# Storing the query and key parts of the first attention by dimension, batch, head and token

## The chip, the cores and the metric

The kernel runs on one NeuronCore of a Trainium2 chip. The metric is the time of one execution on the device, in microseconds (us). The program is one launch with eight layers behind each other (four attentions and four feed-forward layers); the change touches the first of them only.

## The reference, cut to what matters

Eight batches of 512 tokens with 256 features pass through eight layers. The first layer is a causal attention of 16 heads with 16 dimensions each, with scores that also have a term for the relative position:

```
q = (einsum('bsd,ed->bse', layernorm(x), Wq) + bq)  -> [b, head 16, token 512, dim 16]
k, v likewise from the context
QEr  = einsum('bhsd,ld->bhsl', q, Er)
Srel = _skew(QEr)                       # row s is shifted by s
attn = (einsum('bhsd,bhtd->bhst', q, k) + Srel) / sqrt(16)
attn = softmax(where(causal, attn, -inf))
x = x + tanh(gate) * einsum('bhst,bhtd->bhsd', attn, v)
```

Scores are wanted in float32. The kernel gets this from bfloat16 matmuls: each of q and k is split into three bfloat16 parts whose sum is the float32 number, and six products of parts (the list TERMS: 1·1, 1·2, 2·1, 1·3, 3·1, 2·2) are summed in one matmul with a contraction of 6 × 16 = 96 rows.

## The kernel before

The first layer runs as four phases with a barrier of all engines between two of them.

**qkv, "a0" (lines 133 to 373).** Per batch VectorE normalises the tokens, TensorE turns them and multiplies with the weights, and this gives four tiles of 128 features × 512 tokens (two of k, two of q, the list `jobs`). ScalarE copies each with its bias to `q32`. VectorE (`split`, lines 247 to 261) makes three bfloat16 parts of it in five instructions, in one of two buffers `parts[:, j % 2]`. SyncE (`save`, lines 185 to 194) waits for the parts, stores them to device memory with one DMA, 128 partitions × 3 parts × 512 tokens (384 KB), and later stores the values and loads the next context, in the same queue. VectorE may write a parts buffer again when the store of two tiles before has landed (line 254). The tensors in device memory are `q_parts` and `k_parts`, [3, 512, 4096] in bfloat16; a row is one feature (head × 16 + dimension), and a batch is 512 of its 4096 tokens, so a contiguous run of one head, dimension and batch is 1 KB.

**rel_scores, "r0" (lines 1243 to 1360).** GpSimd (POOL) loads the query parts: for each of the six terms one DMA, 16 partitions (the dimensions) × 16 heads × 512 tokens = 256 KB, into rows 16·i to 16·i + 15 of `Q` (line 1273). The loads of two batches may be under way at a time (`q_free`). TensorE multiplies each head with the table Er, VectorE and ScalarE copy the results to one of four buffers `out`, and SyncE stores each head's 640 KB to `rel` (line 1286). A buffer is filled again when its store has landed (lines 1330 and 1351).

**causal_attention, "t0" (lines 3625 to 3887).** SyncE loads the relative scores of a head skewed, in four DMAs of 64 to 256 KB (`relsb`, line 3715). GpSimd loads the query and key parts, six terms × (Q, K) × 256 KB, again 16 partitions each, and the values V, 13 DMAs a batch (line 3756 and 3752). For batch 0 all 13 are issued at the start; for the others one pair is issued after every second head of the batch before (lines 3760 to 3768). GpSimd also adds the mask to the loaded scores and waits for them (`rel{j}`). TensorE's first score matmul waits for all 13 loads (`loaded`). VectorE adds scores and finds the maximum, ScalarE takes the exponential, TensorE turns the tiles and multiplies them with V.

**outproj, "o0".** It isn't touched.

GpSimd's DMAs go through the queue q0 (software), SyncE's through q1 (hardware); both are served by the same 16 DMA engines. The function `attention` (line 377) is edited too, but `program` doesn't call it.

Of the kernel before, what the change touches and what calls it, by code (L numbers as in the profile page):

```python
# [9 lines left out]
BF16 = mybir.dt.bfloat16  # L10
# [5 lines left out]
P = 128  # L16
NB = 8
S = 512
# [114 lines left out]
def qkv(nc, G, name, src, jobs, weights, vjob, ctx=None, affine=None, tile_k=None, nlog=0):  # L133
# [13 lines left out]
    with phase(nc, name, "w c0 c1 c_free stats rstd xn xn_free xt_ps xt_ps_free xt xt_free "  # L147
# [21 lines left out]
        with nc.Block() as block:  # L169

            @block.sync
            def _(sp):

                for c in ("parts_st0", "parts_st1", "v_st0", "v_st1"):
                    sp.sem_inc(s[c], 16)
                for k, (view, shape) in weights.items():
                    sp.dma_start(W[k][tuple(slice(None) for _ in shape)], view).then_inc(s["w"], 16)

                def load(b, p):
                    if ctx is not None:  # L180

                        sp.wait_ge(s["c_free"], b + 1)
                        sp.dma_start(cT[:, p], ctx.rearrange("(k p) t -> p k t", p=P)[:, :, ds(b * S, S)]).then_inc(s[f"c{p}"], 16)

                def save(b, p):
                    for j, (wn, blk, sc, bias, scale, dst, row) in enumerate(jobs):

                        sp.wait_ge(s["parts"], b * nj + j + 1)
                        alone(sp)
                        sp.dma_start(dst.rearrange("r f t -> f r t")[row:row + P, :, ds(b * S, S)],  # L190
                                     parts[:, j % 2]).then_inc(s[f"parts_st{j % 2}"], 16)

                    sp.wait_ge(s["v_sb"], (b + 1) * NVB)
                    sp.dma_start(vdst.rearrange("(t p) d -> p t d", p=P)[:, ds(b * NT, NT), :], vsb[:, p]).then_inc(s[f"v_st{p}"], 16)

                load(0, 0)
                load(1, 1)
                with sp.Fori(0, NB // 2 - 1) as it:
                    for p in range(2):
                        b = it * 2 + p  # L200
                        save(b, p)
                        load(b + 2, p)
                for p in range(2):
                    save(NB - 2 + p, p)

                sp.wait_ge(s["parts_st0"], 16 + 16 * NB * ((nj + 1) // 2))
                sp.wait_ge(s["parts_st1"], 16 + 16 * NB * (nj // 2))
                for p in range(2):
                    sp.wait_ge(s[f"v_st{p}"], 16 + 16 * NB // 2)

# [14 lines left out]
            @block.vector  # L225
            def _(dve):
                ch = Chain(dve, s["dvc"])
                dve.sem_inc(s["q32_free"], 2)

                def rows(b, p, before):  # L230
                    ch.at(before)
                    for t in range(NT):
                        last = nc.vector.bn_stats(st[:, t, :], src[:, ds(b * NT + t, 1), :].rearrange("p o d -> p (o d)"))
                    ch.link(last)
                    alone(dve)
                    for t in range(NT):
                        last = nc.vector.bn_aggr(mv[:, p, t, :], st[:, t, :])
                    last.then_inc(s["stats"], 1)
                    dve.wait_ge(s["rstd"], b + 1)

                    dve.wait_ge(s["xn_free"], b + 1)
                    for t in range(NT):
                        last = nc.vector.tensor_scalar(xn[:, p, t, :], src[:, ds(b * NT + t, 1), :].rearrange("p o d -> p (o d)"),
                                                       mv[:, p, t, 0:1], rstd[:, p, t:t + 1], ALU.subtract, ALU.mult)
                    last.then_inc(s["xn"], 1)

                def split(b, before):
                    ch.at(before)
                    for j in range(nj):

                        dve.wait_ge(s["q32"], b * nj + j + 1)
                        q = q32[:, j % 2, :]
                        k = (nj + 1 - j % 2) // 2
                        dve.wait_ge(s[f"parts_st{j % 2}"], b * (16 * k) + 16 * (j // 2) + 16)
                        ch.link(nc.vector.tensor_copy(parts[:, j % 2, 0, :], q))
                        ch.link(nc.vector.tensor_tensor(r1[:, :], q, parts[:, j % 2, 0, :], ALU.subtract))
                        ch.link(nc.vector.tensor_copy(parts[:, j % 2, 1, :], r1[:, :]))
                        ch.link(nc.vector.tensor_tensor(r2[:, :], r1[:, :], parts[:, j % 2, 1, :], ALU.subtract))
                        ch.link(nc.vector.tensor_copy(parts[:, j % 2, 2, :], r2[:, :]))
                        dve.sem_inc(s["parts"], 1)  # L260
                        dve.sem_inc(s["q32_free"], 1)


                rows(0, 0, 0)
                with dve.Fori(0, NB // 2 - 1) as it:
                    for p in range(2):
                        b = it * 2 + p
                        rows(b + 1, 1 - p, b * link_per_batch + 1)
                        split(b, b * link_per_batch + 2)
                rows(NB - 1, 1, (NB - 2) * link_per_batch + 1)  # L270
                split(NB - 2, (NB - 2) * link_per_batch + 2)
                split(NB - 1, (NB - 1) * link_per_batch + 1)

# [103 lines left out]
def attention(nc, G, name, qs, ks, vs, H, DH, blocks, masks, odst, sums, rel=None):  # L377
# [32 lines left out]
    with phase(nc, name, "in0 in1 loaded qk_free vh vones rel0 rel1 score least expo turned cp_dve cp_act pv "  # L410
# [72 lines left out]
        with nc.Block() as block:  # L483

            @block.gpsimd
            def _(pool):
                with pool.Fori(0, NB // 2) as it:
                    for p in range(2):
# [3 lines left out]
                        for i, (qp, kp) in enumerate(TERMS):  # L492
                            c, r = i // TPC, i % TPC
                            for dst, part, src in ((Q, qp, qs), (K, kp, ks)):
                                pool.dma_start(dst[r * DH:(r + 1) * DH, p, c],
                                               src[part - 1].rearrange("(h d) t -> d h t", d=DH)[:, :, ds(b * S, S)]).then_inc(s[f"in{p}"], 16)
                        pool.dma_start(V[:, p], vs.rearrange("(t p) d -> p t d", p=P)[:, ds(b * NT, NT), :]).then_inc(s[f"in{p}"], 16)

                        pool.wait_ge(s[f"in{p}"], it * (16 * nload) + 16 * nload)
# [743 lines left out]
def rel_scores(nc, G, name, qs, er, rel):  # L1243
# [5 lines left out]
    with phase(nc, name, "er cast erp q0 q1 q_free mm mm_free_a mm_free_v cp_a cp_v st0 st1 st2 st3 dvc") as (s, sb, ps):  # L1249
# [9 lines left out]
        with nc.Block() as block:  # L1259

            @block.gpsimd
            def _(pool):
# [5 lines left out]
                with pool.Fori(0, NB // 2) as it:  # L1268
                    for p in range(2):
                        b = it * 2 + p  # L1270
                        pool.wait_ge(s["q_free"], b + 1)
                        for i, (qp, kp) in enumerate(TERMS):
                            pool.dma_start(Q[i * DH:(i + 1) * DH, p],
                                           qs[qp - 1].rearrange("(h d) t -> d h t", d=DH)[:, :, ds(b * S, S)]).then_inc(s[f"q{p}"], 16)

            @block.sync
            def _(sp):
# [2347 lines left out]
def causal_attention(nc, G, name, qs, ks, vs, rel, odst, sums):  # L3625
# [16 lines left out]
    with phase(nc, name, "in0 in1 loaded rel0 rel1 rel2 rel3 mask masked vones vh score least expo turned cp_dve cp_act pv zero o_free o_st0 o_st1") as (s, sb, ps):  # L3642
# [60 lines left out]
        with nc.Block() as block:  # L3703
# [45 lines left out]
            def _(pool):  # L3749
                def load(p, b, r):  # L3750
# [2 lines left out]
                        return  # L3753
                    qp, kp = TERMS[r]
                    for dst, part, src in ((Q, qp, qs), (K, kp, ks)):
                        pool.dma_start(dst[r * DH:(r + 1) * DH, p], src[part - 1].rearrange("(h d) t -> d h t", d=DH)[:, :, ds(b * S, S)]).then_inc(s[f"in{p}"], 16)

                def batch(it, p, more=True):
                    b = it * 2 + p
# [134 lines left out]
def program(nc, a):  # L3894
    G = Globals()
    with ExitStack() as ctx:
# [11 lines left out]
        G.gate = sb("gate", [P, 8])  # L3908
        G.ones = sb("ones", [1, P])
        G.mhalf = sb("mhalf", [P, 32])  # L3910
        G.qs = dram("q_parts", [3, 512, TOK], BF16)
        G.ks = dram("k_parts", [3, 512, TOK], BF16)
        G.vs = dram("values", [TOK, D])
        G.osT = dram("attended", [D, TOK])
        G.sums = dram("sums", [NB, 16, S])
# [2 lines left out]
        G.kh = dram("k_halves", [2, D, TOK])  # L3918
        G.one_row = dram("one_row", [1, S])
        constants(nc, G, a)  # L3920
        qs, ks = G.qs[:, 0:D, :], G.ks[:, 0:D, :]
        if 0 in STAGES:
            rel = dram("rel", [NB * 16, P * 10 * P])
            qkv(nc, G, "a0", G.X,
# [163 lines left out]
```

## Time and profile before

| | |
|---|---|
| median of 3 runs | 6493.87 us (6456.07 to 6500.29) |
| the profiled execution, own time | 6481.38 us |
| its span (first to last instruction) | 6479.7 us |
| granted TensorE clock, mean | 0.839 |
| PE / DVE / ACT / POOL busy over the span | 72% / 61% / 43% / 31% |
| a0 (projections and splitting) | about 30 to 166 us of the span |
| r0 (relative scores) | about 167 to 459 us |
| t0 (causal attention) | about 459 to 1130 us |

A share of busy time is a mean over the whole program. The change lies in its first 1130 us, so the rows that count are those of windows in this stretch. The DMA share is the mean busy share of the 16 DMA engines.

### The profile page before, as it was taken

Reading aid. Unit: us, or ns where it says so; the run is one execution under the profiler, and the core shown is the slowest. Engines: PE = TensorE matmul, PEld = TensorE weight load, DVE = VectorE, ACT = ScalarE, POOL = GpSimd, SP = SyncE. Lnnn points to the kernel's source line nnn. Section 1 sums busy time; section 2 is a strip of 40 time slices with the busy share of each in tenths; the row PEclk is TensorE's granted clock in tenths of the full one; section 3 lists DMA queues with packets and bytes.
Section 4 is the critical chain, followed back from the end, with each engine's and each line's share of the span. In section 5 each row is a group of like instructions: output and inputs, shape, how many; then the busy total and the mean of one; then the engine's idle time right before and its main releaser. Section 6 shows DMA issues by size and latency. Waiting matters only on the chain. (4 is left out here: it accounts for less than half of the span.)

```text
span 6479.7 us, 102180 instructions
## 1 busy us (share of the span) xinstructions
PE 4692.1 (72%) x24710; PEld 2851.4 (44%) x24710; DVE 3959.5 (61%) x8261; ACT 2814.7 (43%) x5978; POOL 2018.5 (31%) x3020
## 2 busy tenths in 40 slices
PE   7446666391787973797675767697677687995897
PEld 4113333240353322687233645486555574333533
DVE  6335555637546876444387966557866455886565
ACT  2235555114314762322453556434556332772353
POOL 0114443000006641222343554124553113552342
PEclk9557889695897987898777989898889898997897
DMA  4999996100034330210452232002321006332543
GB/s 157 301 323 194 184 185 149 50 0 0 0 115 133 90 75 20 70 43 23 128 157 59 109 113 74 29 7 78 133 74 46 26 16 200 91 86 60 181 124 97
DMA packets 372621, 648.43 MB, mean 100 GB/s; under 512 B 78834, under 2 KB 182931, under 8 KB 372200
## 3 DMA queue, kind: packets, MB, share of 16 engines
q1 hardware_dynamic: 300728, 450.70, 22.9%
q0 software_dynamic: 71488, 193.32, 12.4%
q8 instruction: 133, 2.18, 0.1%
q14 instruction: 272, 2.23, 0.1%
HBM read 373.99 MB, written 238.70 MB: 95 GB/s over the span
## 5 line engine op out<-in xcount | busy, mean ns | idle before, releaser
L1115 DVE TENSOR_REDUCE t_nmax<-t_aps 128x2 f32<-128x1024 f32 x700 | 837.6, 1222 | 281.9 <-PE t_aps L1037 276.4
L1222 ACT ACTIVATE t_expT<-t_bps 128x512 f32<-128x512 f32 x1290 | 701.7, 599 | 288.2 <-PE t_bps L1056 237.8
L1056 PE MATMUL t_bps<-t_Q,t_K 51*128 51x512 f32 (+2 forms) x1290 | 528.9, 472 | 59.4 <-ACT t_expT L1222 43.3
L1037 PE MATMUL t_aps<-t_K,t_Q 49*128 49x512 f32 (+2 forms) x1400 | 467.7, 462 | 64.7 <-DMA t_K<-k_halves 29.4
L1056 PEld LDWEIGHTS t_bps<-t_Q,t_K 51*128 51x128 f32 (+2 forms) x1290 | 230.2, 190 | 528.6 <-ACT t_expT L1222 374.2
L2474 DVE TENSOR_TENSOR f_hl<-f_h,f_hh 128x512 fp32r<-128x512 f32 x192 | 203.9, 1062 | 412.4 <-ACT f_hh L2399 412.4
L3882 ACT ACTIVATE t_relsb<-t_relsb,t_nmax 128x128 f32<-128x128 f32 (+3 forms) x515 | 280.3, 561 | 317.4 <-DVE t_nmax L3855 314.1
L1083 PE MATMUL t_ops<-t_expT,t_V 128*17 128x512 f32 (+1 forms) x2560 | 416.6, 618 | 0.4 <-ACT t_expT L1222 0.4
L3816 PE MATMUL t_tps<-ident,t_relsb 128*128 128x128 f32 x1280 | 266.8, 317 | 173.5 <-ACT t_expT L3701 165.2
L2762 POOL TENSOR_TENSOR a_crossed<-a_qsb,a_tab 128x256 f32<-128x256 f32 x272 | 268.0, 1007 | 299.7 <-ACT a_qsb L2709 272.1
L3855 DVE CUSTOM_DVE_ANT_0 t_relsb<-t_sps,t_relsb 128x128 f32<-128x128 f32 (+3 forms) x515 | 235.5, 485 | 138.2 <-POOL t_relsb L3781 86.5
L3781 POOL TENSOR_TENSOR t_relsb<-t_relsb,t_M 128x128 f32<-128x128 f32 (+1 forms) x384 | 198.9, 547 | 384.8 <-DMA t_relsb<-rel 358.2
L1156 POOL DMA_DIRECT2D t_Q<-q_halves x525 | 272.1, 520 | 141.8 <-POOLq L78 73.3
L3816 PEld LDWEIGHTS t_tps<-ident,t_relsb 128*128 128x128 f32 x1280 | 183.8, 163 | 253.0 <-issue 235.9
L3529 ACT ACTIVATE t_prob<-t_summed,t_nmax 128x256 f32<-128x256 f32 (+1 forms) x560 | 266.0, 480 | 35.3 <-DVE t_nmax L3581 23.4
L1156 POOL DMA_DIRECT2D t_K<-k_halves x525 | 268.7, 514 | 16.4 <-issue 8.9
L3471 PE MATMUL t_tps<-ident,t_prob 128*128 128x128 f32 x964 | 153.9, 306 | 154.3 <-DVE t_prob L3596 154.3
L1037 PEld LDWEIGHTS t_aps<-t_K,t_Q 49*128 49x128 f32 (+2 forms) x1400 | 216.0, 200 | 104.4 <-issue 52.3
L1307 PE MATMUL r_o<-r_erk,r_Q 96*128 96x128 bf16 (+3 forms) x512 | 160.8, 460 | 133.6 <-DVEq L1335 92.4
L3539 ACT COPY t_expT<-t_tps 128x512 f32<-128x512 f32 (+1 forms) x276 | 144.6, 524 | 256.3 <-PE t_tps L3471 256.3
L2339 PE MATMUL f_yps<-f_wdh,f_hh 128*128 128x256 f32 x768 | 217.8, 284 | 13.9 <-DVE f_hl L2474 13.9
L1886 PE MATMUL f1c_ups<-gridT,upT 128*128 x192 | 105.0, 713 | 166.4 <-ACTq L1891 141.0
(431 smaller groups left out, 12493.6 us busy)
## 6 DMA issues: line engine op xcount, KB each, us to landing
rel<-r_out SPq DMA_DIRECT2D x128, 640.0 KB, 5.4
t_relsb<-rel SPq DMA_DIRECT2D x128, 256.0 KB, 4.6
t_Q<-q_halves POOLq DMA_DIRECT2D x420, 64.0 KB, 2.5
t_K<-k_halves POOLq DMA_DIRECT2D x420, 64.0 KB, 2.6
t_relsb<-rel SPq DMA_DIRECT2D x128, 192.0 KB, 3.6
k_halves<-a_parts SPq DMA_DIRECT2D x48, 512.0 KB
q_halves<-a_parts SPq DMA_DIRECT2D x48, 512.0 KB, 5.5
t_relsb<-rel SPq DMA_DIRECT2D x128, 128.0 KB, 3.5
```

The source lines that it names most:

```text
L1037: last = nc.tensor.matmul(aps[:, (t * PPG + i) % 2, x, :], operand(Qr, KA, p, h, slice(t * P, (t + 1) * P)), operand(Kr, KA, p, h, slice(0 ...
L1056: nc.tensor.matmul(bps[:, slot_of(kb, j), :], operand(Kr, KB, p, h, slice(kb * P, (kb + 1) * P)), operand(Qr, KB, p, h, slice(0, S)), star ...
L1083: last = nc.tensor.matmul(ops[j * COL:j * COL + VW, :], V[:, p, kb, g * HG + j, :], expT[:, kb % RING, j, :], start=kb == 0, stop=kb == NT ...
L1115: nc.vector.tensor_reduce(nmax[:, g, t, i * HPT:(i + 1) * HPT], aps[:, (t * PPG + i) % 2], AX.X, ALU.max, negate=True).then_inc(s["maxed"], 1)
L1156: pool.dma_start(dst[o + i * DH:o + (i + 1) * DH, p, cols], rows(src, part, r, g, b)).then_inc(sem, 16)
L1222: nc.scalar.activation(expT[:, kb % RING, j, :], bps[:, slot_of(kb, j), :], ACT.Exp).then_inc(s["expo"], 1 + (PAD if end else 0))
L2339: last = nc.tensor.matmul(o, fast(x), fast(w), start=m == 0 and i == 0 and t % 2 == 0, stop=m == NF - 1 and i == 2, skip_group_check=True)
L2762: last = nc.gpsimd.tensor_tensor(y[:, :, k, :], x[:, :, 1 - k, :], tab[:, 2 * i + 1, t, k * HW:(k + 1) * HW].unsqueeze(1).broadcast_to([P, ...
L3529: nc.scalar.activation(prob[:, u.slot, i, x, 0:w], summed[:, u.slot, i, x, 0:w], ACT.Exp, scale=-1.0, bias=nmax[:, u.slot, i, x:x + 1], ac ...
L3816: last = nc.tensor.transpose(tps[:, u.t % 2, kb * P:(kb + 1) * P], u.tile()[:, kb * P:(kb + 1) * P], G.ident[:, :])
L3855: nc.vector.tensor_tensor_reduce(out=u.tile(), in0=sps[:, u.t, 0:u.w], in1=u.tile(), scale=1.0, scalar=3.0e38, op0=ALU.add, op1=ALU.min, a ...
L3882: nc.scalar.activation(u.tile(), u.tile(), ACT.Exp, scale=-1.0, bias=nmax[:, u.j, u.t:u.t + 1]).then_inc(s["expo"], 1)
```

## The change

The two tensors get the shape [3 parts, 16 dimensions, 8 batches, 16 heads, 512 tokens]. All heads of one dimension and batch now stand behind each other, 16 × 512 × 2 bytes = 16 KB in one piece. A load of one term is then 16 partitions × 8192 elements. The store of a tile, which has 8 heads × 16 dimensions on its 128 partitions, can no longer be written with one access pattern for the three parts, and becomes three DMAs of 128 KB; a run in it is still 1 KB. The semaphores of the stores count 48 a tile where they counted 16.

```
 sp.wait_ge(s["parts"], b * nj + j + 1)
 alone(sp)
-sp.dma_start(dst.rearrange("r f t -> f r t")[row:row + P, :, ds(b * S, S)],
-             parts[:, j % 2]).then_inc(s[f"parts_st{j % 2}"], 16)
+for r in range(3):
+    rows = dst[r].rearrange("d b h t -> b h d t")[ds(b, 1), row // 16:row // 16 + P // 16].rearrange("b h d t -> (b h) d t")
+    sp.dma_start(rows, parts[:, j % 2, r]).then_inc(s[f"parts_st{j % 2}"], 16)
...
-dve.wait_ge(s[f"parts_st{j % 2}"], b * (16 * k) + 16 * (j // 2) + 16)
+dve.wait_ge(s[f"parts_st{j % 2}"], b * (48 * k) + 48 * (j // 2) + 48)
...
 # rel_scores, and likewise causal_attention for Q and K
-pool.dma_start(Q[i * DH:(i + 1) * DH, p],
-               qs[qp - 1].rearrange("(h d) t -> d h t", d=DH)[:, :, ds(b * S, S)]).then_inc(s[f"q{p}"], 16)
+pool.dma_start(Q[i * DH:(i + 1) * DH, p], qs[qp - 1, :, ds(b, 1)].rearrange("d b h t -> d (b h) t")).then_inc(s[f"q{p}"], 16)
...
-G.qs = dram("q_parts", [3, 512, TOK], BF16)
-G.ks = dram("k_parts", [3, 512, TOK], BF16)
+G.qs = dram("q_parts", [3, 16, NB, 16, S], BF16)
+G.ks = dram("k_parts", [3, 16, NB, 16, S], BF16)
```

On SyncE, in the steady loop of a0, a batch before: four stores of parts, then the values and the next context.

```order
L190 DMA k_parts<-a_parts 128x3x512
L188 REGISTER_ALU
L190 ISA
L190 DMA k_parts<-a_parts 128x3x512
L188 REGISTER_ALU
L190 DMA q_parts<-a_parts 128x3x512
L188 REGISTER_ALU
L190 DMA q_parts<-a_parts 128x3x512
```

The same place in the changed kernel:

```order
L192 DMA k_parts<-a_parts 8x16x512
L192 ISA
L192 DMA k_parts<-a_parts 8x16x512
L192 ISA
L192 DMA k_parts<-a_parts 8x16x512
L188 REGISTER_ALU
L192 DMA q_parts<-a_parts 8x16x512 x3
L188 REGISTER_ALU
L192 DMA q_parts<-a_parts 8x16x512 x3
```

Three DMAs stand where one stood, with all else in its place (the second piece begins at the second k tile), and the slowest dimension of the target is 8 (heads) in place of 128.

On GpSimd, the start of t0 before (the first of the six pairs of batch 0, then the end of them with the values):

```order
L3756 DMA t_Q<-q_parts 16x16x512
L3756 DMA t_K<-k_parts 16x16x512
L3752 DMA t_V<-values 128x4x256
```

And in the changed kernel:

```order
L3756 DMA t_Q<-q_parts 16x8192
L3756 DMA t_K<-k_parts 16x8192
L3752 DMA t_V<-values 128x4x256
```

No instruction moved; the shape is one piece of 8192 elements for each of 16 partitions in place of 16 pieces of 512. TensorE, VectorE and ScalarE have the same instructions in the same order.

## Rows read from the trace of the kernel before

**Rows 1.** Stretches of 50 us: busy time by engine, PEclk, DMA share, GB/s.

```profile
core 0: us, PE busy (x) PEld busy (x) DVE busy (x) ACT busy (x) POOL busy (x), PEclk, DMA share, GB/s
100.00:150.00 50.00, 46.33 (x142) 24.38 (x141) 40.13 (x90) 14.70 (x24) 2.76 (x5) 0.93 0.43 139
300.00:350.00 50.00, 28.31 (x91) 9.66 (x92) 20.64 (x47) 17.53 (x47) 3.38 (x6) 0.50 1.02 366
650.00:700.00 50.00, 35.61 (x227) 18.92 (x225) 25.95 (x101) 26.74 (x58) 20.29 (x40) 0.83 0.98 172
```

**Rows 2.** Waits in r0 and, last, in t0: us in total, times, longest.

```profile
ACT r_out L1354 <- DMA rel<-r_out: 157.2, 121, 8.0
PE r_o L1307 <- DMA r_Q<-q_parts: 36.0, 1, 36.0
POOL t_relsb L3781 <- DMA t_relsb<-rel: 287.8, 77, 9.9
```

**Rows 3.** DMA view, 196 to 203 us: only loads of r_Q move.

```profile
DMA packets 249, 0.82 MB, mean 117 GB/s; under 512 B 50, under 2 KB 50, under 8 KB 249
...
q0 software_dynamic: 247, 0.81, 102.2%
q1 hardware_dynamic: 2, 0.01, 1.4%
```

**Rows 4.** DMA view, 205 to 222 us: only stores of rel, from 128 partitions.

```profile
DMA packets 1576, 7.17 MB, mean 422 GB/s; under 512 B 176, under 2 KB 176, under 8 KB 1576
```

**Rows 5.** DMA view, 495 to 500 us in 40 slices: from 497.5 on V and rel.

```profile
DMA  9499829999996979798999799989999999999999
GB/s 213 45 205 139 111 21 152 213 193 188 213 274 188 434 258 451 270 434 299 361 336 369 250 389 332 410 320 357 361 373 332 332 389 336 365 389 373 328 356 426
...
q1 hardware_dynamic: 783, 0.95, 63.3%
q0 software_dynamic: 152, 0.52, 41.0%
```

**Rows 6.** Timeline: start us, us, engine, instruction, idle before it.

```profile
175.72 4.11 POOL L1273 DMA_DIRECT2D r_Q<-q_parts  x7
...
192.93 2.33 PE L1307 MATMUL r_o<-r_erk,r_Q 96*128 96x128 bf16 x8 [36.02 <-DMA r_Q<-q_parts]
...
195.35 42.40 SPq L1286 DMA_DIRECT2D rel<-r_out  x20
...
459.77 0.57 POOL L3756 DMA_DIRECT2D t_Q<-q_parts  x1 [63.94 <-POOLq L78]
...
498.93 1.33 PE L3809 MATMUL t_sps<-t_K,t_Q 96*128 96x128 bf16 x5 [47.69 <-POOLq L3771]
```

**Rows 7.** Exponentials of t0 (L3882) by stretch: ACT busy (x), PEclk, DMA share, GB/s.

```profile
600.00:650.00 50.00, 24.41 (x45) 0.82 0.95 203
650.00:700.00 50.00, 21.31 (x39) 0.83 0.98 172
700.00:750.00 50.00, 22.66 (x43) 0.86 0.89 186
750.00:800.00 50.00, 19.49 (x36) 0.73 0.91 196
800.00:850.00 50.00, 22.00 (x41) 0.86 0.77 170
850.00:900.00 50.00, 21.69 (x40) 0.86 0.95 180
900.00:950.00 50.00, 21.76 (x40) 0.80 0.94 188
1050.00:1100.00 50.00, 24.70 (x46) 0.93 0.55 155
```

**Rows 8.** Groups by line, GpSimd's DMA issues: busy us, mean ns, idle before.

```profile
L1273 POOL DMA_DIRECT2D r_Q<-q_parts x48 | 27.0, 567 | 193.2 <-PEq L1311 192.0 <-issue 0.4
L1267 POOL DMA_DIRECT2D r_erk<-r_pbf x6 | 2.9, 490 | 4.5 <-DVE r_pbf L1321 4.5
```

**Rows 9.** Lines L255 and L190 alone: what VectorE's first cast waits for; the stores.

```profile
  DMA k_parts<-a_parts: 6.0, 15
  DVE a_parts L259: 3.5, 8
...
  DMA q_parts<-a_parts: 0.7, 2
...
L190 SPq DMA_DIRECT2D k_parts<-a_parts x16: 372/372/401, 33.1 to 155.3; - x16
...
DMA to landing us min/median/max: 3.2/3.2/3.9
```

**Rows 10.** DMA view, 117 to 134 us in 40 slices: stores of parts in bursts.

```profile
GB/s 361 267 195 251 328 357 256 15 0 0 0 0 0 0 169 349 349 58 0 0 0 39 342 347 198 0 0 0 0 190 347 347 41 0 0 0 17 332 323 323
```

**Rows 11.** Timeline of a0: VectorE's split beside TensorE, and ScalarE's copy.

```profile
108.09 0.43 DVE L255 CAST a_parts<-a_q 128x512 bf16<-128x512 f32 x1 [0.42 <-DMA k_parts<-a_parts]
...
110.45 1.07 ACT L295 COPY a_xT<-a_xps 128x512 f32<-128x512 f32 x2 [0.23 <-ACT a_vsb L313]
...
111.28 0.43 DVE L255 CAST a_parts<-a_q 128x512 bf16<-128x512 f32 x1 [0.39 <-DMA k_parts<-a_parts]
...
112.80 3.60 PE L356 MATMUL a_jps<-a_xT,a_wq 128*128 128x512 f32 x8
```

More of the change, by code:

```diff
@@ L174, in _ @@
                 for c in ("parts_st0", "parts_st1", "v_st0", "v_st1"):
-                    sp.sem_inc(s[c], 16)
+                    sp.sem_inc(s[c], 48 if c.startswith("parts") else 16)
                 for k, (view, shape) in weights.items():
@@ L204, in _ @@
                     save(NB - 2 + p, p)
-                sp.wait_ge(s["parts_st0"], 16 + 16 * NB * ((nj + 1) // 2))
-                sp.wait_ge(s["parts_st1"], 16 + 16 * NB * (nj // 2))
+                sp.wait_ge(s["parts_st0"], 48 + 48 * NB * ((nj + 1) // 2))
+                sp.wait_ge(s["parts_st1"], 48 + 48 * NB * (nj // 2))
                 for p in range(2):
@@ L495, in _ @@
                                 pool.dma_start(dst[r * DH:(r + 1) * DH, p, c],
-                                               src[part - 1].rearrange("(h d) t -> d h t", d=DH)[:, :, ds(b * S, S)]).then_inc(s[f"in{p}"], 16)
+                                               src[part - 1, :, ds(b, 1)].rearrange("d b h t -> d (b h) t")).then_inc(s[f"in{p}"], 16)
                         pool.dma_start(V[:, p], vs.rearrange("(t p) d -> p t d", p=P)[:, ds(b * NT, NT), :]).then_inc(s[f"in{p}"], 16)
@@ L3755, in load @@
                     for dst, part, src in ((Q, qp, qs), (K, kp, ks)):
-                        pool.dma_start(dst[r * DH:(r + 1) * DH, p], src[part - 1].rearrange("(h d) t -> d h t", d=DH)[:, :, ds(b * S, S)]).then_inc(s[f"in{p}"], 16)
+                        pool.dma_start(dst[r * DH:(r + 1) * DH, p], src[part - 1, :, ds(b, 1)].rearrange("d b h t -> d (b h) t")).then_inc(s[f"in{p}"], 16)
                 def batch(it, p, more=True):
@@ L3920, in program @@
         constants(nc, G, a)
-        qs, ks = G.qs[:, 0:D, :], G.ks[:, 0:D, :]
+        qs, ks = G.qs, G.ks
         if 0 in STAGES:
```

## The prediction, made before the changed kernel ran

> **What bounds the kernel now.** I read the stretches of 50 us first, since the change lies in the first 1130 us only, then the waits in them, then the DMA view of short windows, and the timeline where phases begin. In a0 the DMA engines have room (share 0.43), and TensorE and VectorE are busy for 46 and 40 of 50 us; in r0 the DMA share is 1.02 with TensorE at 28 us; in t0 it is 0.98 in the stretch shown, with no compute engine over 36 us [rows 1]. The waits say the same: in r0 ScalarE waits 157 us for the stores of rel, and TensorE 36 us once for its first query parts; in t0 GpSimd waits 288 of 500 us for the loads of rel [rows 2]. So r0 and t0 are bound by the DMA engines, and the loads that the change reshapes, 48 in r0 and 96 in t0 of 256 KB each, use these engines. The reader is to ask one question: how long does a load hold them, and why?
>
> Alone, the loads move 117 GB/s with the engines' time full (102%), and in the 7 us of that window SyncE's queue moves 2 packets, although its stores are issued from 195.35 us on [rows 3, 6]. Stores of rel alone move 422 GB/s [rows 4]. A load of 262,144 bytes at 117 GB/s holds all 16 engines for 2.24 us. This is the size that the change wants to cut.
>
> **Is it the length of a run?** The change makes runs of 1 KB into runs of 16 KB. If the short run set the 117 GB/s, other transfers with short runs would be slow too. They are not: V goes through the same queue q0, its runs are 256 float32 numbers, also 1 KB, and it lands 128 partitions wide. In the window where it moves (q0's 0.52 MB there are V) beside loads of rel with runs of 512 bytes to 2 KB, the engines reach 332 to 389 GB/s in the steady part [rows 5]. The packets of a query load are also not 1 KB: 0.82 MB in 197 packets of 2 KB or more (249 less 50) is 4.2 KB each, so the trace shows four runs in a packet already [rows 3]. What sets these loads apart is that each writes only 16 partitions, and that their runs in device memory lie 8 KB and 128 KB apart. The first stays in the changed kernel, the second goes. I hold the width for the cause, since it is the only one of the two that a transfer cannot spread over, but the rows don't exclude the other. The Trainium skill, page "SBUF — State Buffer", section "Door 1: The DMA port swizzle", says that the DMA rate depends on how many of 16 ports a transfer's partitions reach, and gives about 109 GB/s as the limit for 16 partitions; by that rule the load stays at 2.4 us whatever its runs are. The trace's 117 GB/s lies close to it, a little above. That page alone can't settle it, since no row here has 16 partitions with long runs.
>
> **The loads, step by step.** The issue on GpSimd: 144 instructions of 567 ns become ones like r_erk's, which have 16 runs and take 490 ns: 144 x 77 ns = 11 us of GpSimd [rows 8]. It counts for nothing, since GpSimd waits 192 us in front of these very issues in r0 [rows 8] and for rel in t0 [rows 2]; without this cover it would be 11 us. The transfers: I take the same 2.24 us, so 0. The bounds are the two rivals below.
>
> **The stores.** One DMA of a tile becomes three. A SyncE issue takes 372 ns, so the last third is issued 0.74 us later; the store lands 3.2 us after its issue now [rows 9]. Its data moves at some 347 GB/s [rows 10], 393,216 bytes in 1.13 us. The trace has no store whose target's slowest dimension is 8. The bounds: if each issue hides under the data of the one before and VectorE's delay under TensorE's slack (below), it costs 0; at the slowest rate of any row, 117 GB/s, the data takes 3.36 us, 2.2 us more, and with the issues the landing is 2.9 us later. I take 1.3 us, near the lower end, because the source stays 128 partitions wide as in the 347 GB/s row. The Trainium skill, page "DMA: Bandwidth & Descriptors", section "Why a DMA increments its semaphore by 16 and not by 1", says that a DMA is spread over the largest number of engines up to 16 that divides the slowest dimension of both sides; that would be 8 here, 1.13 us more per store, and with it 8 x 1.9 = 15 us in place of the 10 below.
>
> Who waits: VectorE's first cast of a tile waits for the store of two tiles before, 17 times in 32, for 6.7 us in all, and when it isn't a store it waits as long for its own chain (3.5 us over 8) [rows 9]. So stores land just in time, in two of four tiles a batch (108.09 and 111.28) [rows 11], and any delay reaches VectorE. A delay of the third tile pushes the fourth too, so a batch pays once: 8 x 1.3 = 10 us. Behind the cast stand ScalarE's copies and TensorE's next tiles; the copy of xT ends at 111.52 and TensorE takes it at 112.80, 1.3 us of slack [rows 11], which could hide all of it if VectorE weren't as tight as TensorE. The last tile's store lands 1.3 us later before the barrier. On SyncE the values and the next context stand behind the stores, up to 0.74 us later a tile; they are wanted a batch later. Sum: 10 + 1.3 = about +12 us, bounds 0 and 8 x 2.9 + 3 = 26 us.
>
> The larger counts of the semaphores and the smaller tensors cost nothing.
>
> **The sum.** 6481.4 (the profiled execution) + 12 = 6493 us. The profiled execution lies 12.5 us under the median of the runs, so for the median it is 6493.9 + 12 = about **6506 us**, no change: about 1% (65 us) is what a measurement of this kernel can tell. The likeliest case alone has 6480 to 6530.
>
> **Rival 1: the run or its place in device memory was the limit; faster.** Then a load moves at V's rate, about 350 GB/s, in 0.75 us, and two thirds of each load's price go. The price from rows: in r0 from the first matmul at 192.93 to the next phase at 459.77 are 267 us [rows 6]; 128 stores of 655,360 bytes at 422 GB/s are 199 us [rows 4]; the other 68 us over the 42 loads that come after the start are 1.6 us each. Two thirds of 42 x 1.6 are 45 us. The start of r0, six loads before TensorE can begin, 6 x 1.49 = 9 us of the 17.2 from issue to matmul [rows 6]. The start of t0, where twelve loads stand ahead of TensorE's first matmul, 39 us after the first issue, 12 x 1.49 = 18 us [rows 6]. The rest of t0: 284 exponentials in the seven stretches with loads, 1.23 us each, against 46 in 50 us (1.09) in the stretch without [rows 7]; 0.145 x 64 = 9.3 us for a batch, 0.78 for each of 12 loads, 65 us for 84, two thirds 43 us. Together 115, less 12 for the stores: -103 us, 6391 us. For it speaks that 117 GB/s is above the page's figure and that reads at a pitch of 8 KB from one narrow DMA occur nowhere else in these rows; against it that V's 1 KB runs are three times as fast. Chance 0.25.
>
> **Rival 2: a 16 KB piece holds an engine until it is done; slower.** Now an engine can turn to SyncE's queue after 4 KB. That the price of a load is 1.6 us in r0 and 0.78 in t0, under the 2.24 for which it moves, shows that stores and loads of rel share in this time. If the row of 16 KB becomes one packet, they don't. r0: 42 x 0.64 = 27 us. t0: 84 x 1.46 = 123 us at most, half of it (61) since the share of the DMA engines is 0.77 to 0.98 and not full [rows 7]. With the stores +100 us: 6594 us. It decides as soon as packets of q0 are larger than 8 KB. For it speaks that in rows 3 the other queue is starved already with twelve loads waiting; the same speaks against it, as there is little left to lose. Chance 0.13.
>
> **That the change doesn't do what it says** is excluded by the shapes in the two kernels' orders: 16x8192 in place of 16x16x512.
>
> **How the numbers follow.** Forecast 0.62, rival 1 0.25, rival 2 0.13. Within 1% (6429 to 6559) is the forecast; faster by over 1% is rival 1, 0.25; slower is rival 2, 0.13. The range leaves out the far half of each rival: 6380 to 6585.
>
> **What would show it.** Right: loads alone still move 110 to 125 GB/s with a full share; TensorE's wait for r_Q stays 34 to 37 us and that for the first scores of t0 46 to 49 us; r0 lasts 285 to 295 us from phase to phase; VectorE's wait for stores of parts grows from 6.7 to 15 to 25 us, and a0 is some 12 us longer. Wrong: a rate of over 200 GB/s in a window with q0 alone, and t0 with over 43 exponentials per 50 us (rival 1); packets over 8 KB in q0 and a longer wait of GpSimd for rel (rival 2); a wait of VectorE over 40 us in a0.

## The result, and the profile after

The changed kernel takes **6524.91 us**, the median of 10 runs (6505.33 to 6543.68), beside 6490.44 us (6456.07 to 6514.83) for the kernel before on the same chip. The ratio is 1.0061 with a 95% interval from 1.0045 to 1.0077: some 34 us slower, which is clear of the scatter (the interval leaves out 1), within the 1% that was forecast as no change, and 19 us over the point. The number is near; one term of its sum is not.

The span falls apart at three instructions: GpSimd's issue of r_er (r0 begins), its first issue of t_Q (t0 begins), and SyncE's first load of o_rs (the output projection).

| us | a0 | r0 (of it up to the first matmul) | t0 (up to the first scores) | the rest | span |
|---|---|---|---|---|---|
| before | 167.4 | 292.4 (25.5) | 672.7 (39.2) | 5347.2 | 6479.7 |
| after | 182.2 | 300.7 (24.3) | 682.6 (34.8) | 5376.5 | 6542.0 |
| difference | +14.8 | +8.3 | +9.9 | +29.3 | +62.3 |

The change touches the first three columns, and their +33 us are what the medians show. The rest runs the same code; by the medians its +29 belong to this one execution, which was 19 us above its own median while the profiled one of before was 9 below. Over all twelve profiles of this text the rest takes 5343 to 5378 us. So the phases are compared, and not the spans; each phase is still one profile of its kernel, and its own scatter is told below from groups of kernels.

The timeline of the changed kernel, four places where phases begin (start us, us, engine, line, instruction, idle before it and its releaser); beside them [rows 6]:

```profile
182.23 0.74 POOL L1264 DMA_DIRECT2D r_er<-in_L_xattn_Er  x1 [36.60 <-POOLq L78]
206.53 2.33 PE L1307 MATMUL r_o<-r_erk,r_Q 96*128 96x128 bf16 x8 [39.41 <-DMA r_Q<-q_parts]
482.89 0.49 POOL L3756 DMA_DIRECT2D t_Q<-q_parts  x1 [65.86 <-POOLq L78]
517.68 1.33 PE L3809 MATMUL t_sps<-t_K,t_Q 96*128 96x128 bf16 x5 [43.24 <-POOLq L3771]
```

From the issue of t_Q to the first scores are 34.8 us, where [rows 6] have 39.2: twelve loads alone have become a little shorter (34.8 to 36.6 us in the six kernels below with long packets in t0, 38.0 to 39.2 in the four with short ones). The issue of one takes 0.49 us in place of 0.57.

The stretches of 50 us, with the columns of [rows 1]:

```profile
100.00:150.00 50.00, 42.38 (x135) 22.32 (x134) 35.87 (x86) 11.37 (x18) 3.81 (x6) 0.96 0.46 142
300.00:350.00 50.00, 30.98 (x99) 10.15 (x97) 22.21 (x50) 18.84 (x50) 5.84 (x12) 0.50 1.00 352
650.00:700.00 50.00, 34.07 (x211) 18.42 (x205) 24.03 (x97) 25.79 (x57) 21.69 (x43) 0.82 0.75 183
```

In a0 TensorE gets through 135 matmuls in 50 us where it did 142. The DMA share is 0.46: nothing there is out of transfer capacity, so I looked for a wait. The waits, first of what stands at the head of VectorE's tile (line L256, us in total and times, as in [rows 9]), then of r0, and of t0 from 520 to 1020 us (us in total, times, longest). The row of t0 in [rows 2] is from 500 to 1000; the two stretches begin 37 and 40 us behind the first issue of t_Q.

```profile
  DMA k_parts<-a_parts: 17.6, 15
  DVE a_parts L260: 3.5, 8
...
  DMA q_parts<-a_parts: 1.8, 2
```

```profile
ACT r_out L1354 <- DMA rel<-r_out: 165.5, 119, 11.5
POOL t_relsb L3781 <- DMA t_relsb<-rel: 295.5, 76, 9.5
```

Three things grew: VectorE's wait for stores of parts from 6.7 to 19.4 us; ScalarE's wait for stores of rel from 157.2 to 165.5, and with it the longest one from 8.0 to 11.5; GpSimd's wait for loads of rel from 287.8 to 295.5, with the longest as it was (9.9 and 9.5). The last two pay in phases whose transfers of rel did not change.

**The loads alone.** The DMA view of the changed kernel from 193 to 207 us, in which only r_Q is loaded (GB/s in 40 slices, then the packets):

```profile
GB/s 94 281 0 47 47 281 94 281 0 47 47 234 140 281 0 47 47 187 187 281 0 0 47 234 187 281 0 0 47 234 164 234 47 47 47 234 140 281 47 0
DMA packets 209, 1.71 MB, mean 122 GB/s; under 512 B 104, under 2 KB 104, under 8 KB 104
...
q0 software_dynamic: 208, 1.70, 99.9%
```

122 GB/s where [rows 3] have 117. The run is sixteen times as long, its place in device memory is another, and the rate stays. The packets did change: of q0's 208, 104 are under 512 bytes, and the other 104 carry nearly all of the 1.70 MB, 16 KB each. A row now travels as one packet where four went before.

**The stores alone.** The same view from 120 to 125.5 us (busy tenths and GB/s in 40 slices), where stores of parts are all that moves; beside it the kernel before in a like stretch, 104 to 112 us:

```profile
DMA  0000015434554454455555532100004453555455
GB/s 0 0 0 0 0 52 89 52 67 164 186 194 149 127 127 134 149 186 201 164 186 194 201 119 75 45 0 0 0 0 97 60 67 82 209 194 179 134 149 149
```

```profile
DMA  0000000299999400000000006999981000000000
GB/s 0 0 0 0 0 0 0 87 353 353 348 333 358 133 0 0 0 0 0 0 0 0 0 0 225 343 333 369 353 302 41 0 0 0 0 0 0 0 0 31
```

The digit is mostly 4 or 5 where it was 9, and the rate 127 to 201 GB/s inside a burst where it was about 350: what half of the 16 engines would give, each at its usual pace. The view is a mean and doesn't name engines. The Trainium skill, page "DMA: Bandwidth & Descriptors", section "Why a DMA increments its semaphore by 16 and not by 1", says that a DMA is spread over the largest number of engines up to 16 that divides the slowest dimension of both sides, here 8; by that rule the trace agrees. Nor are the issues what they were; SyncE's line L192 (ns: minimum, median and maximum):

```profile
L192 SPq DMA_DIRECT2D k_parts<-a_parts x48: 598/624/813, 33.8 to 169.2; - x48
L192 SPq DMA_DIRECT2D q_parts<-a_parts x48: 598/606/617, 41.7 to 176.4; - x48
```

One issue takes 606 to 624 ns where the whole tile's took 372, so three of them hold SyncE for 1.8 us a tile.

### The profile page after: what moved, and what is told of

It is laid out like the page before. It is cut to its first block and busy times, and to the rows that moved or that the text cites. A ratio compares the mean times of both kernels' runs of the same rounds, so it can differ in the third digit from the quotient of the medians.

```text
span 6542.0 us, 102316 instructions
## 1 busy us (share of the span) xinstructions
PE 4729.9 (72%) x24710; PEld 2873.4 (44%) x24710; DVE 3962.3 (61%) x8261; ACT 2814.9 (43%) x5978; POOL 2009.1 (31%) x3020
## 5 line engine op out<-in xcount | busy, mean ns | idle before, releaser
L1057 PE MATMUL t_bps<-t_Q,t_K 51*128 51x512 f32 (+2 forms) x1290 | 529.5, 471 | 59.2 <-ACT t_expT L1223 43.2
L3882 ACT ACTIVATE t_relsb<-t_relsb,t_nmax 128x128 f32<-128x128 f32 (+3 forms) x515 | 279.4, 560 | 325.5 <-DVE t_nmax L3855 322.3
L3471 PE MATMUL t_tps<-ident,t_prob 128*128 128x128 f32 x964 | 156.7, 310 | 154.3 <-DVE t_prob L3596 154.1
```

The lines of the kernel that those rows point to most:

```text
L1057: nc.tensor.matmul(bps[:, slot_of(kb, j), :], operand(Kr, KB, p, h, slice(kb * P, (kb + 1) * P)), operand(Qr, KB, p, h, slice(0, S)), star ...
L3882: nc.scalar.activation(u.tile(), u.tile(), ACT.Exp, scale=-1.0, bias=nmax[:, u.j, u.t:u.t + 1]).then_inc(s["expo"], 1)
```

## The experiments

Ten more kernels ran. The question was what the 33 us consist of, and why long runs brought nothing.

**split_only**: the kernel before, with its store cut in three and the old layout kept.

```diff
-sp.dma_start(dst.rearrange("r f t -> f r t")[row:row + P, :, ds(b * S, S)],
-             parts[:, j % 2]).then_inc(s[f"parts_st{j % 2}"], 16)
+for r in range(3):
+    sp.dma_start(dst[r, row:row + P, ds(b * S, S)], parts[:, j % 2, r]).then_inc(s[f"parts_st{j % 2}"], 16)
```

> The kernel before, with its old layout, but each tile's store made as three DMAs (one part each, 128 partitions x 512) in place of one. Before, a0 lasted 167.4 us up to the next phase's first load; the changed kernel's 182.2. Theory A (the target's slowest dimension of 8 makes the store slow, by fewer DMA engines): three DMAs with 128 rows cost only their two extra issues of about 0.37 us; SyncE's issue stays at 372 ns, a0 is 168 to 174 us and VectorE's waits for the stores of parts 7 to 12 us in all. Theory B (the number of DMAs is what costs): a0 180 to 184 us, waits 17 to 21 us as in the changed kernel. In both r0 and t0 stay at 292 and 673 us within 4 us, and the whole is within 0.3% of before (A) or 0.2% above it (B).

Measured: 6489.07 us, ratio 1.0011 [0.9992, 1.0029]; a0 168.1 us (+0.7), VectorE's waits for stores 6.0 and 0.7 us, as before to the tenth. Three stores in place of one cost nothing by themselves (the waits did not even reach the 7 to 12 us expected): the delay comes from their target. Its line L191 shows the ordinary price of an issue:

```profile
L191 SPq DMA_DIRECT2D k_parts<-a_parts x48: 332/333/617, 33.6 to 156.7; - x48
L191 SPq DMA_DIRECT2D q_parts<-a_parts x48: 332/382/452, 40.3 to 163.0; - x48
```

**four_buffers**: the changed kernel with four buffers of parts, one to each tile of a batch, so that a store has a whole batch to land.

```diff
-parts = sb("parts", [P, 2, 3, S], BF16)
+parts = sb("parts", [P, 4, 3, S], BF16)
...
-dve.wait_ge(s[f"parts_st{j % 2}"], b * (48 * k) + 48 * (j // 2) + 48)
+dve.wait_ge(s[f"parts_st{j}"], b * 48 + 48)
```

> The changed kernel with four buffers for the parts in place of two, so that VectorE waits for the store of a whole batch before. If a0's 14.8 us more come from VectorE's wait for the landing of stores, a0 falls to 160 to 168 us, below before even, and the wait is nearly 0. If they come from the stores' own time on SyncE or the DMA engines (a queue that falls behind), a0 stays over 176 us. r0 and t0 stay at 301 and 683 us within 4 us. The whole: 15 to 22 us less than the changed kernel in the first case, none in the second.

Measured: 6518.44 us, 1.0052 [1.0032, 1.0071]; a0 169.2 us, r0 296.4, t0 684.0. The slow stores are all still there (606 to 619 ns an issue), VectorE waits for none, and 13.0 of the 14.8 us of a0 are back: they were the wait. a0 is not shorter than before, as I had expected (160 to 168), though the 6.7 us of before are gone too; that wait was covered by something else, and TensorE's 46 of 50 us in [rows 1] left little to win. t0 keeps its loss and r0 half of it (296.4, where 301 within 4 was expected), so there is a second cause. The whole does not show the 13 us: 15 to 22 us less than the changed kernel were expected, the two ratios, 1.0052 and 1.0061, differ by 6 us, and their intervals overlap. With four runs of this kernel only the phase carries the reading.

**padded_heads**: the changed kernel with 32 unused elements behind each head's tokens, so that a row of a load is sixteen runs of 1 KB again. Stores and order of the layout stay.

```diff
-G.qs = dram("q_parts", [3, 16, NB, 16, S], BF16)
+G.qs = dram("q_parts", [3, 16, NB, 16, S + 32], BF16)
...
-qs, ks = G.qs, G.ks
+qs, ks = G.qs[:, :, :, :, 0:S], G.ks[:, :, :, :, 0:S]
```

> The changed kernel with 32 elements of padding behind each head's 512 tokens, so that a load is again 16 x 16 runs of 1 KB, at nearly the same places. The stores are unchanged. Theory A (the 16 KB packets hold an engine, and cost the 8.3 us of r0 and 9.9 us of t0): the packets of q0 are 4 KB again, r0 is 290 to 295 us, t0 670 to 676 us; a0 stays at 182. The first stores of rel behind the loads come sooner. Theory B (the pitch of 128 KB between the 16 rows in device memory costs them): r0 and t0 stay at 301 and 683 us. By both the loads alone still move 115 to 125 GB/s, since they write 16 partitions. The whole: 6500 to 6512 us by A, as the changed kernel by B.

**dim_major_tiles**: the reverse. The weights' columns are put in the order dimension, then head, on the way in; parts are stored as [3, batch, 256, token], so that a store keeps 128 rows as its slowest dimension, while a load is sixteen rows of 16 KB as in the change.

```diff
-G.qs = dram("q_parts", [3, 512, TOK], BF16)
+G.qs = dram("q_parts", [3, NB, D, S], BF16)
...
-qs[qp - 1].rearrange("(h d) t -> d h t", d=DH)[:, :, ds(b * S, S)]
+qs[qp - 1, ds(b, 1)].rearrange("b (d h) t -> d (b h) t", d=DH)
```

> The features of q and k come out of the projection ordered by dimension and head (the columns of the weights are laid out so), and the parts are stored as [3, batch, dimension, head, token]: a tile's store is one DMA of 128 partitions x 3 x 512 as before the change, and a load is sixteen rows of 16 KB behind each other (256 KB in one piece). a0 should be 167 us within 2, with SyncE's issue 0.37 us. r0 and t0: 301 and 683 us if the 16 KB packets cost there, 292 and 673 if the 128 KB pitch did (it is 16 KB here). The load's rate stays at 115 to 125 GB/s by the theory of the 16 partitions; over 200 if the place in device memory set it. The whole: 0.3% above before in the first case, the same in the second.

Both together are the test of the second cause:

| | runs, ratio | a0 | r0 | t0 |
|---|---|---|---|---|
| after (slow stores, 16 KB rows) | 6524.91, 1.0061 | 182.2 | 300.7 | 682.6 |
| padded_heads (slow stores, 1 KB runs) | 6495.7, 1.0015 [0.9999, 1.0031] | 183.2 | 289.6 | 664.5 |
| dim_major_tiles (good stores, 16 KB rows) | 6512.31, 1.0041 [1.0021, 1.0061] | 166.9 | 301.6 | 687.0 |
| before (good stores, 1 KB runs) | 6490.44 | 167.4 | 292.4 | 672.7 |

Each cause comes and goes by itself: a0 follows the store's target, r0 and t0 follow the row of 16 KB. It is not the pitch between rows: padded_heads keeps it about (136 KB for 128) and loses the cost, dim_major_tiles has 16 KB and keeps the cost. The whole DMA view from 0 to 1500 us says what the row changes; first q0 of the changed kernel, then of padded_heads, then of dim_major_tiles:

```profile
q0 software_dynamic: 5984, 42.08, 16.9%
```

```profile
q0 software_dynamic: 12896, 42.08, 17.3%
```

```profile
q0 software_dynamic: 5984, 42.08, 17.0%
```

The same 42.08 MB, in 6912 packets fewer: 144 loads of 48 packets less, 16 of 16 KB for 64 of 4 KB. The engines' time is the same too, so over the whole the loads did not become dearer for the engines; the work beside them did. A burst of six loads beside stores of rel shows it, 20 us of the DMA view, first after (237 to 257 us), then padded_heads (239 to 259); begun at the first issue instead, the same two stretches give the same shares within 0.1%:

```profile
q1 hardware_dynamic: 933, 4.23, 62.3%
q0 software_dynamic: 192, 1.57, 39.4%
```

```profile
q1 hardware_dynamic: 1120, 5.09, 72.6%
q0 software_dynamic: 480, 1.57, 30.6%
```

In both 1.57 MB of loads go through; beside them 4.23 MB of rel with long packets and 5.09 with short ones (4.62 in the kernel before, over its own 20 us). In this burst q0's share is higher too, 39.4% against 30.6%. The longest stall is visible on VectorE in the changed kernel, behind such a burst; 7.8 us were the longest before:

```profile
253.31 0.89 DVE L1333 COPY r_out<-r_o 128x128 f32<-128x128 f32 x2 [11.32 <-DMA rel<-r_out]
```

One such stall is not the loss: in dim_major_tiles, which loses as much, the longest is 8.9 us. The totals are. In padded_heads ScalarE's wait goes back:

```profile
ACT r_out L1354 <- DMA rel<-r_out: 154.3, 121, 8.4
```

It is 154.3 to 157.2 us in the four kernels with short packets, and 162.9 to 167.7 in the three with long ones at this width. GpSimd's wait for rel in t0, in 500 us that begin 40 us behind each kernel's first issue of t_Q, is 280.9 to 289.1 us in the four with short packets (280.9 in padded_heads), and 292.7 to 302.1 in the six with long ones.

That a 16 KB packet keeps an engine from the other queue until it is through is my reading of these rows; no row shows an engine's choice. That the packet's length costs this much is shown.

**wide_128, wide_64, wide_32**: the changed kernel, with each of r0's loads of 256 KB sent to 128, 64 or 32 partitions instead of 16, at the same number of bytes. The query data land in other places than the product needs, so these three do not compute the reference; they only measure. For 32 partitions:

```diff
-pool.dma_start(Q[i * DH:(i + 1) * DH, p], qs[qp - 1, :, ds(b, 1)].rearrange("d b h t -> d (b h) t")).then_inc(s[f"q{p}"], 16)
+x = qs[qp - 1, :, ds(b, 1)].rearrange("d b h t -> d (b h) t")
+pool.dma_start(Q[i // 2 * 32:i // 2 * 32 + 32, p, i % 2 * 8:i % 2 * 8 + 8], bass.AP(x.tensor, x.offset, [[8 * S, 32], [S, 8], [1, S]])).then_inc(s[f"q{p}"], 16)
```

> The changed kernel, with the loads of r_Q in r0 alone made 128 partitions wide: each moves 256 KB as before, from one piece in device memory, to 128 partitions x 2 KB of a Q tile of 128 partitions. It computes relative scores from other query data, so its output is not the reference's; the work of the engines is the same. The changed kernel's loads move 122 GB/s alone, and r0 lasts 300.7 us, 24.3 of them before the first matmul. Theory of the width: the loads alone move 300 to 400 GB/s, the first matmul comes 15 to 18 us into r0, and r0 is 235 to 255 us. Theory of the place in device memory or of the queue q0: the rate stays under 150 GB/s and r0 over 290 us.

> As the run with 128 partitions, with 64 partitions x 4 KB a load (rows 0 to 63 for the first four loads, 64 to 127 for the last two); other query data too. If the rate follows the number of partitions: about 122 x 4, so as fast as 128 wide, r0 235 to 260 us. If it follows the ports by the Trainium skill's map (SBUF — State Buffer, Door 1), where 64 partitions in a row reach no more ports than 32: 190 to 230 GB/s alone, and r0 250 to 270 us, as with 32.

> As the run with 128 partitions, with 32 partitions x 8 KB a load; other query data too. Twice the width of the changed kernel: 190 to 240 GB/s alone by the theory of the width, r0 250 to 272 us. Under 150 GB/s and over 290 us if the width isn't what limits.

One run each: 6469.76, 6490.91 and 6465.38 us beside 6471.62, also one run, for the kernel before. One run says little of a whole; what counts here is r0 and its windows. What the DMA view says of a window with only these loads (packets, MB, mean rate) in wide_128 (192 to 198 us), wide_64 and wide_32 (192 to 199 us):

```profile
DMA packets 571, 1.90 MB, mean 317 GB/s; under 512 B 108, under 2 KB 108, under 8 KB 570
```

```profile
DMA packets 467, 1.57 MB, mean 224 GB/s; under 512 B 84, under 2 KB 84, under 8 KB 467
```

```profile
DMA packets 285, 1.57 MB, mean 224 GB/s; under 512 B 94, under 2 KB 94, under 8 KB 94
```

| partitions of a load | 16 | 32 | 64 | 128 |
|---|---|---|---|---|
| GB/s alone | 122 | 224 | 224 | 317 |
| r0 | 300.7 | 262.6 | 261.0 | 254.6 |

This is the limit that the run was suspected to be. Twice the partitions are 1.8 times the rate, 64 are no better than 32, and r0 loses 38 us at the first step. Not all of the 38 are the width, since a row of a load becomes shorter with it (8 KB, 4 KB, 2 KB): wide_64, whose packets are 4 KB, is at 261.0 us, and the four kernels with 16 partitions and 4 KB packets are at 289.6 to 292.7, so the width alone is worth some 30 us. At 16 partitions the packet's length leaves the rate alone where it is (117 and 122 GB/s), so the rates in the table are the width's. That 64 partitions equal 32 is odd unless one knows which ports they reach: the Trainium skill, page "SBUF — State Buffer", section "Door 1: The DMA port swizzle", gives 16, 32 and 64 partitions 104, 189 and 196 GB/s as measured for 1 MiB. The trace agrees in the order, and lies above these figures by a seventh to a fifth.

**good_layout**: dim_major_tiles with a padded head (fast stores and short runs) and four buffers, the three findings put together at the old width.

> Three measured parts together: features ordered by dimension and head (store in one DMA of 128 rows), 32 elements of padding behind each head (packets of 4 KB), and four buffers for the parts. Expected by the single runs: a0 155 to 163 us (166.9 less VectorE's 7 us of waits), r0 288 to 293 (289.6 with padding), t0 662 to 668 (664.5). Against before (167.4, 292.4, 672.7) 12 to 24 us less: 6465 to 6478 us if before is 6488. If padding helped only because of the changed stores, r0 and t0 are as before and the whole is 7 us less.

Measured: 6484.9 us beside 6482.81, ratio 1.0000 [0.9981, 1.0019]; a0 166.6, r0 291.7, t0 670.8. A miss: it is the kernel before, in every phase within 2 us. VectorE waits for no store here, and a0 is 0.8 us shorter. The 6.7 us of waiting in [rows 9] were never to be had, as four_buffers had hinted.

**six_slots_96_wide** and **six_slots_unpadded**: the width put to use in a kernel that computes the reference. The loads are narrow because each of the six 16-row slots of the stacked operand is fetched apart. Here SyncE stores a part once per slot that wants it (six slots in device memory for three parts, by a broadcast source), and a load fetches all 96 rows at once: one DMA a batch in r0, and eight of 96 partitions and four heads in t0. The first has the padded head (runs of 1 KB), the second hasn't (16 KB rows in r0, 4 KB in t0).

```diff
-TERMS = ((1, 1), (1, 2), (2, 1), (1, 3), (3, 1), (2, 2))
+TERMS = ((1, 1), (1, 2), (1, 3), (2, 1), (2, 2), (3, 1))
+SLOTS = {"wq": ((0, 0, 3), (1, 3, 2), (2, 5, 1)), "wk": ((0, 0, 3), (0, 3, 2), (0, 5, 1))}
...
+for first, slot, n in SLOTS[wn]:
+    src = parts[:, j, first:first + n] if wn == "wk" else parts[:, j, first:first + 1].broadcast_to([P, n, S])
+    sp.dma_start(dst.rearrange("b r f t -> f r b t")[row:row + P, slot:slot + n, ds(b, 1)].rearrange("f r b t -> f r (b t)"),
+                 src).then_inc(s[f"parts_st{j}"], 16)
...
-for i, (qp, kp) in enumerate(TERMS):
-    pool.dma_start(Q[i * DH:(i + 1) * DH, p],
-                   qs[qp - 1].rearrange("(h d) t -> d h t", d=DH)[:, :, ds(b * S, S)]).then_inc(s[f"q{p}"], 16)
+pool.dma_start(Q[:, p], qs[ds(b, 1)].rearrange("b r (d h) t -> (b r d) h t", d=DH)).then_inc(s[f"q{p}"], 16)
...
+pool.dma_start(dst[0:KR, p, r * 4:r * 4 + 4], src[ds(b, 1)].rearrange("b r (d h) t -> (b r d) h t", d=DH)[:, r * 4:r * 4 + 4])
...
-G.qs = dram("q_parts", [3, 512, TOK], BF16)
+G.qs = dram("q_parts", [NB, 6, D, S + 32], BF16)
```

> The theory of the width put to use. The six terms' parts are stored six times in device memory, [batch, 6 terms, dimension, head, token + 32], by three DMAs of 128 rows a tile (twice the bytes), with four parts buffers and features ordered by dimension and head; the terms are taken in another order. r0 loads a batch's queries by one DMA of 96 partitions, t0 by four DMAs of 96 partitions x 4 heads for Q and K each. By the width: the loads alone move 280 to 380 GB/s, the start of r0 (25.5 us) and of t0 (39.2 us) fall by 7 to 10 and 14 to 22 us; r0 240 to 260 us, t0 590 to 640 us; a0 158 to 175 us, since stores move twice the bytes. The whole 6370 to 6430 us, 1 to 1.8% under before. If the width isn't the limit: r0 290 us, t0 665 to 675 us, and the whole as before or up to 15 us over.

> The run with six slots and loads of 96 partitions, without the padding, so that a row of a load is one piece: 16 KB in r0, 4 KB in t0. It asks whether the long piece costs when it goes to many partitions. With padding a0 was 167.6 us, r0 262.1, t0 607.6. If what a 16 KB piece costs is that the other queue must wait while an engine writes it slowly (a port shared by four engines), it costs little here, where an engine writes fast: r0 within 4 us of 262, t0 within 8 us of 608. If a long piece costs of itself, r0 is 267 to 275 us as between the narrow kernels with 1 KB and 16 KB runs (8.3 us), and t0, whose pieces are 4 KB, is unchanged. The whole 6385 to 6405 us either way.

Measured: **6396.27 us, ratio 0.9850 [0.9818, 0.9882]**, and 6408.34 us beside 6496.57, 0.9859 [0.9824, 0.9894]. Phases (a0, r0, t0): 167.6, 262.1, 607.6 and 168.5, 266.6, 606.6 us. Both beat both kernels by more than 1%. r0 gained 30 us (262.1, where 240 to 260 were expected) and t0 65, of which 16 are its start (23.5 us in place of 39.2). Storing twice the bytes cost nothing, since the engines had room in a0: the share rises to 0.69 and a0 stays at 167.6 us. (TensorE's 148 matmuls in the stretch below, against 142, are no gain: four_buffers and good_layout have 148 too.) The same stretches as above, of six_slots_96_wide:

```profile
100.00:150.00 50.00, 46.95 (x148) 24.36 (x147) 40.54 (x91) 14.89 (x24) 2.53 (x4) 0.97 0.69 234
300.00:350.00 50.00, 31.86 (x102) 10.52 (x100) 22.71 (x52) 19.31 (x52) 1.95 (x2) 0.50 1.00 393
700.00:750.00 50.00, 34.12 (x226) 18.40 (x225) 26.19 (x107) 27.94 (x63) 21.19 (x41) 0.90 0.59 161
```

393 GB/s in r0 at a full share, where [rows 1] have 366: I read this as the same engines with less of their time on slow writes. The padding is worth 4.6 us in r0 and nothing in t0, one profile of each, and the two ratios overlap; 266.6 us lie between what either theory of the packets expected (within 4 of 262, or 267 to 275), and the whole of six_slots_unpadded came out 3 us over its range. With wide loads the packet's length is not settled.

One expectation failed outright. The 96-wide loads alone were to move 280 to 380 GB/s. From 178 to 184 us, first six_slots_96_wide, then six_slots_unpadded:

```profile
DMA packets 312, 1.28 MB, mean 213 GB/s; under 512 B 0, under 2 KB 0, under 8 KB 312
```

```profile
DMA packets 92, 1.49 MB, mean 248 GB/s; under 512 B 1, under 2 KB 1, under 8 KB 1
```

The engines' time is full in both (97.5% and 102.9%), and 96 partitions move no more than 32 or 64 do, give or take a tenth. So six times the partitions brought 1.8 and 2.0 times the rate, as the step from 16 to 32 did; why they bring no more is open. These kernels also issue fewer DMAs (one for six in r0, eight for twelve in t0). In r0 the wide kernels, which keep 48 loads, show that the width does it by itself; for t0 the two were not taken apart.

## Why the prediction was right or wrong

- **What bounds the loads: right.** The width of 16 partitions was held for the limit, 2.24 us a load and a term of 0. The loads alone went from 117 to 122 GB/s, inside the 110 to 125 named, and the widths measured by themselves confirm the cause. Rival 1, at 6391 us, falls: no window with q0 alone has a mean over 200 GB/s until the partitions grow, and the seven stretches of t0 with loads have 39.4 exponentials in 50 us on the mean (40.6 before), where it asked for over 43. (Two readings behind it were loose. The 332 to 389 GB/s "of V" are V and loads of rel together, so no row had V's own rate; and 249 less 50 packets are 199, not 197, so 4.1 KB each.) The start of t0 got 4.4 us shorter and r0's 1.2; that is all of it. TensorE's waits moved with other things: for r_Q 39.4 us (34 to 37 forecast), since TensorE is idle from 15.1 us ahead of r_er's issue and not from 10.5, while VectorE catches up with its waits; four_buffers, with the same stores and no such wait, has 35.2. GpSimd's idle time ahead of r_er has grown as well, from 32.0 to 36.6 us; for the first scores 43.2 (46 to 49 forecast), for the shorter start.
- **GpSimd's issue, 11 us hidden: right.** 0.49 us in place of 0.57, and nothing came of it.
- **The stores, +12 us: right in place, small in size.** VectorE's wait went to 19.4 us (15 to 25 forecast), a0 by 14.8. The step "I take 1.3 us, near the lower end, because the source stays 128 partitions wide" was wrong: half the engines, and issues that take 606 to 624 ns. The value beside it, 15 us by 8 engines, was the better one. That the wait is what lengthens a0 was shown by four_buffers, in that phase; its whole is too coarse for it.
- **The step that failed: the loads' term of 0 beside other work.** I made rate and price one thing: same rate, same price. Rival 2 said what else could change, and named its point: "as soon as packets of q0 are larger than 8 KB". They are 16 KB. The mechanism is there, in r0 with 8.3 of the forecast 27 us, and in t0 with about 14 of 61. r0 is 300.7 us, past the 285 to 295 named as a sign of being right; the three kernels with long packets at 16 partitions have 296.4 to 301.6, the four with short ones 289.6 to 292.7. For t0 I take the six kernels with long packets (676.4 to 691.3, mean 684.8) against the four with short ones and narrow loads (664.5 to 673.5, mean 670.4); the groups don't overlap, though a single kernel can lie 8 us from its group's mean. Its price was too high because it took all sharing for lost; in the changed kernel SyncE's queue still has 62% of the engines' time through a burst. The 27 and 61 were worked out from the old price per load against the full 2.24 us, an upper bound used as a value.
- **The sum.** 14.8 (stores) + 8.3 (r0) + 9.9 (t0) = 33 us against the 12 forecast; the medians differ by 34. The likeliest case's own range, 6480 to 6530, held it with 5 us to spare, because a second cost was left out. The point looks near because the program is long: of the change's own 34 us it had 12.

Open: what the extra 1.8 us of a0 in four_buffers are (the last tile's slow landing before the barrier is near this size, 1.3 us forecast; it was not isolated), why an engine's turn costs the other queue what it does, and why 96 partitions move no more than 32.

## What to carry to other kernels

Ask first how many partitions a transfer touches on its narrow side, and only then how long its runs are: here sixteen times the run was worth nothing to the loads, and twice the partitions 1.8 times the rate, worth it even where the bytes had to be stored twice to get there. But measure each step: 64 and 96 partitions brought little over 32. A layout is paid for at both ends: a store whose target had a slowest dimension of 8 moved at about half the rate of one with 128, and a piece that became one packet of 16 KB was not free where another queue shared the engines. And where two kernels' phases can be told apart in the trace, compare phases, since one execution's span was 29 us off here in code that nobody touched.

## What was not expected of the hardware

- A DMA with a target of 8 × 16 × 512 takes SyncE 606 to 624 ns to issue, against 333 to 382 for the same bytes with 128 rows (medians of 48 instructions each). What in the shape costs it was not taken apart.
- Loads of 96 partitions alone move 213 and 248 GB/s at a full share, loads of 32 and of 64 move 224, and loads of 128 move 317.
- A row of sixteen separate runs of 1 KB travels in four packets of 4 KB, and a whole row in one of 16 KB. In padded_heads 64 unused bytes between the runs are enough to turn the one into the other (12896 packets against 5984).
- A wait that is seen in a profile (VectorE, 6.7 us in a0) can be worth nothing when taken away: a0 is 169.2 and 166.6 us without it, and 167.4 with it.
